# A feed-forward layer with ternary weights: one fp32 product, or two bf16 products of a high and a low part

## The reference

```
def _ternary(w):
    scale = jnp.maximum(jnp.mean(jnp.abs(w)), 1e-08)
    w_t = jnp.clip(jnp.round(w / scale), -1.0, 1.0)
    return w + jax.lax.stop_gradient(w_t - w)
h = jnp.einsum('bsd,fd->bsf', x, _ternary(W1)) + b1      # 256 -> 1024
h = jax.nn.gelu(h, approximate=False)
out = jnp.einsum('bsf,df->bsd', h, _ternary(W2)) + b2    # 1024 -> 256
...
x = _layernorm(x + _L0_ffn_ref(x, ...), axis=-1)
```

## Time and profile before

| | |
|---|---|
| median of 3 runs | 2068.15 us (2067.75 to 2072.11) |
| the profiled execution's own time | 2071.29 us |
| its span, first to last instruction | 2069.2 us |
| PE busy | 1540.5 us (74%) |
| DVE busy | 1080.2 us (52%) |
| ACT busy | 651.7 us (31%) |
| POOL busy | 385.5 us (19%) |
| mean granted clock of PE | 0.864 |

### The profile page before, as it was taken

The page is one execution under the profiler, slowest core; times in us unless marked ns, Lnnn a source line. Parts: engine busy times, 40 slices in busy tenths (PEclk is TensorE's granted clock), DMA queues, the critical chain, the costliest instruction groups (busy, mean ns, idle before and its releaser), DMA issues. The chain is left out here.

```text
span 2069.2 us, 46585 instructions
## 1 busy us (share of the span) xinstructions
PE 1540.5 (74%) x19736; PEld 1274.7 (62%) x19740; DVE 1080.2 (52%) x2377; ACT 651.7 (31%) x1403; POOL 385.5 (19%) x414
## 2 busy tenths in 40 slices
PE   2897885879678577978857797886612399999980
PEld 1595664549567455966744596665412388888870
DVE  4775438477642837764283776427413144344434
ACT  2522313352132244313224432322310244344430
POOL 0013113111311302041130204023042300000006
PEclk9897997989789788989978898898855699999995
DMA  6012101021111102121110212111042486677633
GB/s 235 12 55 62 43 21 51 22 62 45 62 42 32 51 12 62 44 73 33 41 41 22 62 44 66 39 31 31 22 125 87 130 261 213 226 239 236 222 112 117
DMA packets 165450, 174.98 MB, mean 85 GB/s; under 512 B 10529, under 2 KB 130209, under 8 KB 164897
## 3 DMA queue, kind: packets, MB, share of 16 engines
q1 hardware_dynamic: 154688, 154.33, 23.5%
q10 hardware_dynamic: 7520, 9.77, 1.3%
q0 software_dynamic: 3072, 8.39, 1.3%
HBM read 126.58 MB, written 45.88 MB: 83 GB/s over the span
## 5 line engine op out<-in xcount | busy, mean ns | idle before, releaser
L1620 POOL TENSOR_TENSOR e_parts<-e_whole,e_parts 128x512 bf16<-128x512 f32 x96 | 111.7, 1165 | 739.4 <-ACT e_parts L1614 739.1
L1989 PE MATMUL m_bank<-e_xT,e_w 128*128 128x256 bf16 x2208 | 245.5, 273 | 0.6 <-DVE e_xT L2067 0.6
L1989 PEld LDWEIGHTS m_bank<-e_xT,e_w 128*128 128x128 bf16 x2208 | 216.4, 98 | 26.3 <-DVE e_xT L2067 0.9
L668 PE MATMUL bank<-arena 64*64 64x64 f32 (+2 forms) x6400 | 203.7, 222 | 0.1
L668 PEld LDWEIGHTS bank<-arena 64*64 64x64 f32 x6400 | 203.1, 134 | 0.4 <-issue 0.2
L2080 DVE TENSOR_TENSOR e_h<-m_bank,e_silu 128x256 f32<-128x256 f32 x184 | 78.2, 425 | 201.9 <-ACT e_silu L2032 201.9
L2001 PE MATMUL m_bank<-m_xT,e_h 128*128 128x256 bf16 x1104 | 124.1, 273 | 0.0
L2001 PEld LDWEIGHTS m_bank<-m_xT,e_h 128*128 128x128 bf16 x1104 | 108.0, 98 | 12.2
L2032 ACT ACTIVATE e_silu<-m_bank 128x256 f32<-128x256 f32 x184 | 70.5, 383 | 124.1 <-PE m_bank L1989 124.1
L948 POOL TENSOR_TENSOR rstd<-ve,neghalf 128x2 f32<-128x2 f32 x48 | 33.8, 703 | 354.0 <-DVE ve L927 354.0
L940 DVE TENSOR_TENSOR y<-bank,res 128x512 f32<-128x512 f32 x32 | 22.0, 688 | 135.2 <-PE bank L540 135.1
(11 more groups left out here) (296 smaller groups left out, 3223.1 us busy)
## 6 DMA issues: line engine op xcount, KB each, us to landing
e_w<-parts SPq DMA_DIRECT2D x92, 512.0 KB, 5.4
e_whole<-E SPq DMA_DIRECT2D x96, 256.0 KB, 3.0
parts<-e_parts SPq DMA_DIRECT2D x192, 128.0 KB, 2.8
m_xT<-parts SPq DMA_DIRECT2D x46, 512.0 KB, 7.7
slots<-zeros SPq DMA_DIRECT2D x4, 1536.0 KB, 6.8
back<-e_y ACTq DMA_DIRECT2D x23, 256.0 KB, 6.5
e_x<-slots SPq DMA_DIRECT2D x22, 256.0 KB, 6.6
w_rest<-W_rest SPq DMA_DIRECT2D x1, 3584.0 KB, 25.4
```

The source lines that it names most:

```text
L668: last = pe.matmul(b[r, p * width:(p + 1) * width], lhs[r, 4 * g + p, :], rhs[r, 4 * g + p, :], start=True, stop=True)
L1620: pool.tensor_tensor(out=e_parts[:, j % 2, LOW], in0=e_whole[:, j % 2], in1=e_parts[:, j % 2, HIGH], op=ALU.subtract).then_inc(sem("e_low" ...
L1989: last = pe.matmul(bank[b][:, col:col + SLOTS], w[:, wp, c, f * P:(f + 1) * P], xeT[u][:, xp, c, :], start=j == 0, stop=j == len(terms) - 1)
```

## The change

The ternary matrices are loaded into stream 1's arena, and the last of the three setup operations writes -1, 0, 1 to two bf16 tensors. The copy of d_xT on ACT now writes the high part of x in bf16 (`xb`), and DVE subtracts it from the bank to make the low part, which is what now empties the bank. ff1 multiplies each ternary block with both parts. In each quarter ACT, after the two Gelus, waits for them and casts the quarter of `h` to its high part; DVE makes the low part. ff2 is cut into four quarters as well, with stages 201 to 201.75, each of which waits for its low part; the token tile is now its innermost loop, and the bank is claimed at the first quarter. New semaphores are `f_half`, `f_high` and `f_low`.

```diff
--- before.py
+++ after.py
@@ -152,7 +152,8 @@
              "n_weights_split": 8, "n_shift": 2 * PINV_ITERS, "n_zeros": 1, "n_exp2": 1, "n_a": 1, "n_answers": 1,
              "n_vones": 1, "n_gz": 1,
              "d_high": 2, "d_neg": 1, "d_values": 2, "d_o": 1, "d_zeros": 1, "d_logs": 1, "d_weights": 2,
-             "g_high": 4, "g_zeros": 1, "g_neg": 1, "g_cos": 4, "g_sum": 4}
+             "g_high": 4, "g_zeros": 1, "g_neg": 1, "g_cos": 4, "g_sum": 4,
+             "f_half": 1, "f_high": 4, "f_low": 4}
 
 
 
@@ -233,7 +234,7 @@
     "k": {"coef": (F32, NC * BRANCHES)},
     "oT": {"n": (F32, NC * T)},
 }
-FFN = {"h": (F32, FC, T)}
+FFN = {"xb": (BF16, 2, NC, T), "h": (F32, FC, T), "hb": (BF16, 2, FC, T)}
 MEMORY = {"v": (F32, NT, D), "s0": (F32, H1, T), "s1": (F32, H1, P), "r": (F32, NC, T)}
 GATED = {
     "sum": (F32, 4, NC, T), "v": (F32, KT2, D), "p": (F32, NC, GROUPS32, KT2, T),
@@ -355,17 +356,20 @@
                 at += w
             return whole, views
 
-        W, whole_W = {"ff1": sb("w_ff1", [P, NC, FF])}, {}
+        W, whole_W = {}, {}
         for group, names in GROUPS.items():
             whole_W[group], views = side_by_side("w_" + group, {n: MATRICES[n] for n in names}, rows=NC)
             W.update(views)
-        w2 = sb("w_ff2", [P, FC, D])
+        ternary = [sb("w_ff1", [P, NC * FF], BF16), sb("w_ff2", [P, FC * D], BF16)]
         whole_bias, bias = side_by_side("biases", COLUMNS)
         whole_rows, rows = side_by_side("rows", {n: D for n in ROWS})
         width = max(words_of(table) for table in (NYSTROM, DILATED, FFN, MEMORY, GATED))
         arenas = [sb(f"arena{s}", [P, width]) for s in range(STREAMS)]
 
         scratch = arenas[0][:, 0:1024]
+        drawn = [arenas[1][:, i * NC * FF:(i + 1) * NC * FF] for i in range(2)]
+        ff1 = ternary[0][:].rearrange("p (c n) -> p c n", c=NC)
+        ff2 = ternary[1][:].rearrange("p (c n) -> p c n", c=FC)
 
         tables_of_shapes = shape_constants()
         whole_consts, consts = {}, {}
@@ -417,7 +421,8 @@
         with nc.Block() as block:
             loaded = {n: sem("load_" + n) for n in ("ternary", "tables", "act", "nystrom", "rest")}
             columns_of = lambda n: a["W_" + n].rearrange("(c p) n -> p c n", p=P)
-            order = [(W["ff1"][:], columns_of("ff1"), "ternary"), (w2[:], columns_of("ff2"), "ternary")]
+            order = [(drawn[i].rearrange("p (c n) -> p c n", c=c), columns_of(n), "ternary")
+                     for i, (n, c) in enumerate((("ff1", NC), ("ff2", FC)))]
             order += [(whole_W[n][:], columns_of(n), n) for n in GROUPS]
             early = [(whole_bias[:, 0], a["B"]), (whole_consts["early"][:, 0], a["C_early"])]
             order2 = [(whole_consts[n][:, 0], a["C_" + n]) for n in ("fp32", "bf16")] + [(whole_rows[:, 0], a["R"])]
@@ -475,13 +480,11 @@
                 link(dve.tensor_scalar(small[:, 8:12], small[:, 4:8], -1.0, None, ALU.mult))
 
                 dve.wait_ge(loaded["ternary"], 32)
-                for i, w in enumerate((W["ff1"], w2)):
-                    flat = w[:].rearrange("p c n -> p (c n)")
+                for i, flat in enumerate(drawn):
                     link(dve.tensor_reduce(small[:, 16 + i:17 + i], flat, axis=AX.X, op=ALU.add,
                                            apply_absolute_value=True))
                 dve.wait_ge(pe_step, 1)
-                for i, w in enumerate((W["ff1"], w2)):
-                    flat = w[:].rearrange("p c n -> p (c n)")
+                for i, flat in enumerate(drawn):
                     c = small[:, 20 + 4 * i:24 + 4 * i]
                     link(dve.tensor_scalar(c[:, 0:1], psum[0][:, i:i + 1], small[:, 63:64], 1e-8, ALU.mult, ALU.max))
                     link(dve.reciprocal(c[:, 1:2], c[:, 0:1]))
@@ -489,7 +492,8 @@
                         f = flat[:, half * 1024:(half + 1) * 1024]
                         link(dve.tensor_scalar(f, f, c[:, 1:2], None, ALU.mult))
                         link(dve.tensor_scalar(scratch, f, -0.5, -1.0, ALU.is_lt, ALU.mult))
-                        link(dve.scalar_tensor_tensor(f, f, 0.5, scratch, ALU.is_gt, ALU.add))
+                        link(dve.scalar_tensor_tensor(ternary[i][:, half * 1024:(half + 1) * 1024], f, 0.5, scratch,
+                                                      ALU.is_gt, ALU.add))
                 dve.wait_ge(act_step, 2 + H1)
                 link(dve.tensor_tensor(dec0[:], dec0[:], keep[:, None, :].to_broadcast([P, H1, T]), ALU.mult))
                 link(dve.tensor_tensor(dec1[:], dec1[:], keep[:, None, 0:P].to_broadcast([P, H1, P]), ALU.mult))
@@ -1197,7 +1201,8 @@
             b = bk.await_filled(act, "d_coef12")
             act.copy(n["coef"][:, NC * T:], b[:, 0:NC * (P + M)]).then_inc(bk.emptied("d_coef12"), 1)
             yield 133
-            act_norm(act, bat, "d_xT")
+            b = bk.await_filled(act, "d_xT")
+            act.copy(v["f"]["xb"][:, HIGH].rearrange("p c t -> p (c t)"), b[:]).then_inc(sem(f"f_half{s}"), 1)
 
         def pool_dilated(pool, bat):
             s, v, bk = bat % STREAMS, st[bat], st[bat]["bk"]
@@ -1222,7 +1227,7 @@
 
         def pe_ffn(pe, bat):
             s, v, bk = bat % STREAMS, st[bat], st[bat]["bk"]
-            n, x = v["f"], x_of(bat)
+            n = v["f"]
             yield 200
             bk.await_emptied(pe, "d_xT")
             for i in range(FC // 2):
@@ -1231,19 +1236,28 @@
                 for j in range(2):
                     f = 2 * i + j
                     for c in range(NC):
-                        last = pe.matmul(b[:, j * T:(j + 1) * T], W["ff1"][:, c, f * P:(f + 1) * P], x[:, c, :],
-                                         start=c == 0, stop=c == NC - 1)
+                        for part in (HIGH, LOW):
+                            last = pe.matmul(b[:, j * T:(j + 1) * T], ff1[:, c, f * P:(f + 1) * P], n["xb"][:, part, c, :],
+                                             start=c == part == 0, stop=c == part == 1)
                 last.then_inc(bk.filled(f"f_h{i}"), 1)
-            yield 201
             for i in range(FC // 2):
-                bk.await_emptied(pe, f"f_h{i}")
-            pe_tokens(pe, bat, "f_out", w2, 0, n["h"], FC)
+                yield 201 + i / 4
+                pe.wait_ge(sem(f"f_low{s}"), due("f_low", bat, i + 1))
+                if i == 0:
+                    b = bk.claim(pe, "f_out")
+                for f in (2 * i, 2 * i + 1):
+                    for part in (HIGH, LOW):
+                        for t in range(NT):
+                            last = pe.matmul(b[:, t * D:(t + 1) * D], n["hb"][:, part, f, t * P:(t + 1) * P], ff2[:, f, :],
+                                             start=f == part == t == 0, stop=f == FC - 1 and part == LOW and t == NT - 1)
+            last.then_inc(bk.filled("f_out"), 1)
             yield 202
             pe_norm(pe, bat, "2", "f_xT")
 
         def act_ffn(act, bat):
             s, v, bk = bat % STREAMS, st[bat], st[bat]["bk"]
             n = v["f"]
+
             yield 200
             for i in range(FC // 2):
                 yield 200 + i / 4
@@ -1252,10 +1266,24 @@
                     f = 2 * i + j
                     last = act.activation(n["h"][:, f, :], b[:, j * T:(j + 1) * T], ACT.Gelu, bias=bias["ff1"][:, f:f + 1])
                 last.then_inc(bk.emptied(f"f_h{i}"), 1)
+                bk.await_emptied(act, f"f_h{i}")
+                act.copy(n["hb"][:, HIGH, 2 * i:2 * i + 2, :], n["h"][:, 2 * i:2 * i + 2, :]).then_inc(sem(f"f_high{s}"), 1)
             yield 202
             act_norm(act, bat, "f_xT")
 
         def dve_ffn(dve, bat, link):
+            s, v, bk = bat % STREAMS, st[bat], st[bat]["bk"]
+            n = v["f"]
+            yield 200
+            b = bk.await_filled(dve, "d_xT")
+            dve.wait_ge(sem(f"f_half{s}"), due("f_half", bat, 1))
+            dve.tensor_tensor(n["xb"][:, LOW].rearrange("p c t -> p (c t)"), b[:],
+                              n["xb"][:, HIGH].rearrange("p c t -> p (c t)"), ALU.subtract).then_inc(bk.emptied("d_xT"), 1)
+            for i in range(FC // 2):
+                yield 200.1 + i / 4
+                dve.wait_ge(sem(f"f_high{s}"), due("f_high", bat, i + 1))
+                dve.tensor_tensor(n["hb"][:, LOW, 2 * i:2 * i + 2, :], n["h"][:, 2 * i:2 * i + 2, :],
+                                  n["hb"][:, HIGH, 2 * i:2 * i + 2, :], ALU.subtract).then_inc(sem(f"f_low{s}"), 1)
             yield 201
             dve_residual_norm(dve, bat, link, "f_out", "2")
```

## The result

The changed kernel takes 2021.59 us in the median of 4 runs (2020.77 to 2026.46), the kernel before 2068.38 (2067.75 to 2072.11, 4 runs): ratio 0.9775, 95% interval 0.9756 to 0.9794, 46.8 us less. The forecast was 2026. One execution of the kernel before, in the last of the later jobs, took 3269.63 us and is left out of the comparisons. The profiled execution took 2020.77 us, with a span of 2018.8 and a mean granted clock of 0.860 (before 2071.29, 2069.2 and 0.864).

A forecast was written before the change was run, and what follows sets the result against it. TensorE alone was taken to bound the feed-forward layer. Gains of 10.3+10.5+10.2+11.0 = 42 us took the profiled 2071.3 us to 2029, or 2026 against the median; own range 2018 to 2034 (chance 0.83), wider range 2014 to 2040.

The forecast's parts named there:

- The bound before: Feed-forward layer before the change: TensorE alone is the bound, back to back; batch 1's add at S+29.35, S being ff1's start.
- PE's terms: TensorE in the layer: 7.1 us each for ff1 and ff2 per pair, plus 1.2 to 2.4 us for low clock.
- ACT's terms: Gelus and casts on ACT: eight quarters of 1.39 us from S+2.65, the last low part on DVE at S+14.65.
- Level course: PE and ACT run level through the layer; batch 0's add starts between S+14.75 and S+15.8.
- The new wait: Layer's tail: batch 1's norm queues behind batch 0's on DVE, some 3 us on the path; its add at S+18.7.
- What was counted as nothing: Setup, head, weight-piece stream, stages after the layers and the clock behind the layer: put at nothing.
- Setup and head: Setup loads and the new subtraction after the d_xT copy cost nothing; with the fast clock up to 0.6 us.
- Clock behind the layer: Low clock after batch 1's transposes may last longer: -1 to +1.5 us each, put at nothing, +-6 us in all.
- (a): Rival: PE stays at 1.2 GHz through the layer, no gain there, 2067 to 2078 us; chance 0.04.
- (b): Rival: on ACT, Gelu and the cast evict each other's table, 8 us later per pair, 2100 us; chance 0.02.
- (c): Rival: low clock reaching into the next layer and quarters of 1.54 us give back 10 us, 2036 us; chance 0.11.

The follow-up runs named there:

- e5: The changed kernel with ff2 alone in bf16, ff1, its weights and x staying fp32: 2051.18 us, ratio 0.9909 to the kernel before.
- e3: The changed kernel with a second cast of every quarter on ACT into a spare tensor nobody reads: 2037.45 us, ratio 0.9826 to the kernel before.
- e9: The changed kernel with a one-column Gelu on ACT behind batch 0's d_xT copy, so the table load comes early: 2023.92 us, ratio 0.9757.
- e10: The early one-column Gelu of e9 added to e2: 2024.03 us, ratio 0.9763 to the kernel before.
- e7: The changed kernel with batch 0's four quarters before batch 1's and the low parts of h on POOL: 2021.11 us, ratio 0.9756.
- e8: The changed kernel with batch 0's four quarters before batch 1's, low parts staying on DVE: 2026.27 us, ratio 0.9777 to the kernel before.
- The controls: The changed kernel run again unedited in two later jobs: 2025.55 and 2025.41 us, ratios 0.9776 and 0.9765 to the kernel before.
- e2: The changed kernel with the low parts' products left out on PE, low parts still made: 2020.57 us, ratio 0.9748 to the kernel before.
- e6: The changed kernel with the low parts of h made on POOL instead of DVE, same batch order: 2030.69 us, ratio 0.9793.

## Why the prediction was right

**The bound before.** That PE's queue alone set the end of the layer was right: with both halves' matmuls cheaper, batch 1's add moved from S+29.35 to S+18.43 in the mean. Forecast S+18.7 in three pairs and 19.3 in the fourth, 18.85 in the mean. The latest was the third pair, not the fourth: how long ff1 stays at the low clock (it took 9.45 us there) moves the end more than the weight cast does.

**PE's terms.** ff2 takes 7.15 us (e5, and the third pair of after), forecast 7.1. ff1 takes 8.11 to 9.45 us, forecast 8.3 to 9.5: 8.61 in the mean, so the low clock at the head costs 1.5 us a pair, where 1.2 to 2.4 was allowed. PE is busy 15.36 to 16.44 us of each stretch; 14 to 16 was said.

**ACT's terms.** The quarter of 1.39 us came out exactly, and the cast in it costs 0.52 by e3 (0.51 forecast). Start at S+2.66 (S+2.65), last low part done at S+14.59 (S+14.65). The weight cast in the fourth pair puts its add 0.51 us later, S+15.02 against 14.51. ff2 begins on PE at S+7.94, at the cast of ACT's fourth quarter (S+8.5 and the fifth or sixth were said), and meets a short wait (0.34 us) only for the last in the first pair and for the last two in the fourth, none in the others; the forecast had it just behind ACT, with gaps of some tenths.

**Level course.** The forecast had batch 0's add at S+14.75 to 15.8, whichever of the two is last. Measured S+14.51, 14.84, 15.61 and 15.02. The first is ACT's floor and lies 0.24 us below the range; the third is PE's, at its upper end, because PE ran at the low clock for (1 - 0.88) x 2 x 19.04 = 4.6 us of that stretch. e9 and e10 show both limits one by one. Here the sum was off in size: I took S+15.25, and 15.85 in the fourth pair, 15.4 in the mean, and the mean was 15.0. That is 1.6 us over the four pairs, and with the norms 3.43 apart (3.45 forecast) it makes the layer's gain 43.7 us instead of 42.

**The new wait.** That batch 1's norm is queued behind batch 0's held; put at some 3 us on the path, it was somewhat less: its add comes 2.2, 2.6, 2.6 and 2.2 us after PE's last matmul. e7 and e8 show that this is DVE's order, and e7's second and third pair (S+16.47 against e8's 17.93 and 17.95) that 1.5 us a pair were to be had.

**What was counted as nothing.** Setup and head: ahead of the first S the two kernels took 210.14 and 208.10 us, apart by less than that stretch varies (207.7 to 214.2 over the profiles). Clock behind the layer: in the first pair, over the 3.6 us from the start of batch 1's transposes, it was 0.53 before and is 0.50:

```profile
270.90:274.50 3.60, 3.42 (x10) 2.93 (x11) 0.13 (x1) 0.59 (x1) 1.04 (x1) 0.50 0.00 0
```

Over 12 us from that start the clock was 0.87, 0.75, 0.76 and 0.86 before, and 0.85, 0.85, 0.81 and 0.76 after, which is 18.2 us at the low level over the four pairs before and 17.5 after. So nothing was given back there.

**What the sum left open.** 43.7 of the 46.8 us between the medians are the layer's. The controls are 45.9 and 48.3 us below the kernel before in their jobs, with 44.4 and 43.7 in the layer. So some 1.5 to 4.6 us more were gained than the layer shows. The three profiles of the changed kernel took 1904.3, 1907.6 and 1910.9 us outside of the layer, the one of the kernel before 1911.1; it may be that later stages meet a better clock, or chance. No run here separates that. The median lies 4.4 us below the forecast; 1.7 of them are the layer's, and the rest is this open part. So it moved the median away from the forecast and isn't what made it come true.

**The rivals.** (a) PE stays at 1.2 GHz: out, the clock was 1.00 all through ff2, with the short wait in it:

```profile
256.81:264.57 7.76, 7.42 (x66) 6.01 (x63) 4.53 (x8) 6.32 (x14) 1.16 (x1) 1.00 0.00 0
```

Its mechanism is real all the same. Where PE idled 0.78 us in each 1.39 (e10, and e2 in two pairs), the clock did fall within ff2. The Trainium skill ("TensorE: Matmul & The Clock Gate", section "A second HAM failure mode: psum-queue depth-cycling") describes it in a bf16 kernel that idles briefly between matmul groups; by that rule the clock should swing in e10, and it did. The changed kernel, with gaps of at most 0.34 us in ff2, and e3, with gaps of 0.86 beside longer groups, kept the clock at 1.00, so the page's words don't say by themselves which kernel is such a case. (b) Eviction of the table: out, there are four loads for the Gelus, as before, and none between the Gelus and casts. The Trainium skill ("ScalarE: Activation LUTs", section "What ACT_TABLE_LOAD costs") adds about 1.38 us of drain to a load; here the measurement decides, and no such drain was on the path: the load begins at 250.24, 0.02 us after the cast before it ends, the first Gelu follows 0.01 us after the load, and in e10, without the load there, that Gelu starts 1.41 us earlier than in e2, 0.13 more than the load's 1.28. (c) Part given back: out in both its terms. The low clock behind the layer took no more than before (above). The slower subtractions beside POOL exist (the first two take 2.08 us together, not 1.38), but PE was in ff1 then and no one waited; nor did quarters take 1.54.

## What to carry to other kernels

When a matmul phase is the bound and gets cheaper, list the chains beside it with their period and their head: here PE let batch 0's add start at S+14.5 (e9's second pair), and ACT's 2.65 + 8 x 1.39 us and the low part behind it ended at S+14.6, so making one of them cheaper was worth 0.2 us a pair and both 1.6. Follow each queue in order before pricing a part of a change: e5 was mispriced by 16 us because the later half's work stood behind the earlier half's on PE. Where two streams share an engine, a norm that used to lie under the other stream's matmuls comes onto the path once these are short. Here the order on that engine (low parts of batch 1 before the add of batch 0) was then what cost: freeing DVE of them without a change of order (e6) gained nothing, with it (e7) some 5 us.
